# Two groups of two graphs ahead of fifteen groups of four in a five-engine graph kernel

## What is computed

```python
# per graph: x [128,128], adj [128,128]
e      = leaky_relu((x * a_0) @ x.T, 0.2)
scores = where(adj == 1, e, -9e15)
y      = layernorm(x + softmax(scores) @ x)
h      = y @ W_loop.T
g      = h @ Wg_loop.T
vals   = (h + b_loop) * sigmoid(g + bg_loop)
out    = layernorm(y + relu(adj.T_is_1 @ vals))
```

## Time and profile before

| | us |
|---|---|
| median of 3 runs | 109.68 |
| lowest and highest run | 109.47, 110.07 |
| the profiled execution, its own time | 109.15 |
| its span, first to last instruction | 107.4 |
| first real product's weight load | 5.28 |
| first score work on DVE (relu of group 0) | 7.12 |
| last product of the neighbour sums ends | 101.3 |
| mean granted TensorE clock, share of full | 0.99 |

### The profile page before, as it was taken

One profiled execution on the slowest core, in us unless ns is written; L12 is line 12 of the kernel. 1 busy time (PEld: TensorE's weight loads), 2 busy tenths in 40 slices (PEclk: granted clock), 3 DMA queues, 4 the chain that ended last, 5 costly groups with the idle time before them and its releaser, 6 DMA issues.

```text
span 107.4 us, 2765 instructions
## 1 busy us (share of the span) xinstructions
PE 97.9 (91%) x677; PEld 89.4 (83%) x684; DVE 94.4 (88%) x380; ACT 87.1 (81%) x217; POOL 81.0 (75%) x158
## 2 busy tenths in 40 slices
PE   6998999999999999999999999999999999799600
PEld 6986787889999999999999999999999999677400
DVE  0159999999998999997989999999799999987990
ACT  3159968999999999699999999888998889868100
POOL 5025555597588879999989899998979898986760
PEclk9999999999999999999999999999999999999995
DMA  0899999999910093707893304620200303331524
GB/s 15 307 407 367 373 350 297 352 350 388 330 53 0 5 294 95 195 0 201 278 312 97 98 9 113 180 72 26 73 27 6 98 6 98 98 98 46 156 77 124
DMA packets 22531, 17.36 MB, mean 162 GB/s; under 512 B 1265, under 2 KB 18418, under 8 KB 22514
## 3 DMA queue, kind: packets, MB, share of 16 engines
...
q10 hardware_dynamic: 288, 0.26, 0.8%
...
## 4 chain that ended last, share of the span: by engine, by line
POOL 38%; DVE 23%; issue 18%; PE 14%; ACT 3%; POOLq 1%; DVEq 0%; ACTq 0%
POOL rs L707 9%; POOL cent L740 8%; POOL rs L743 7%; DVE nscore L936 5%; DVE res L947 5%; PE p_ag L1038 4%; PE p_hg L1111 3%; DVE rel L918 2%; POOL minus L704 2%; POOL out_s L753 2%; POOL rs L731 2%; PE p_e L1054 2%; POOL rs L702 2%; DVE out_s L1005 2%; POOL y L722 2%
## 5 line engine op out<-in xcount | busy, mean ns | idle before, releaser
L1111 PE MATMUL p_hg<-w_both,y_t 128*128 128x256 f32 x128 | 30.6, 381 | 0.9 <-ACT y_t L871 0.9
L1111 PEld LDWEIGHTS p_hg<-w_both,y_t 128*128 128x128 f32 x128 | 23.0, 190 | 3.8 <-ACT y_t L871 1.3
L830 ACT ACTIVATE prob<-nscore,nmax 128x128 f32<-128x128 f32 x64 | 20.2, 396 | 1.0 <-DVE nmax L936 1.0
L947 DVE SCALAR_TENSOR_TENSOR res<-p_o,rz,inputs 128x128 f32<-128x128 f32 x64 | 18.0, 344 | 1.3 <-ACT y L847 0.6
L1083 PE MATMUL p_o<-inputs,prob_t 128*128 128x129 f32 x128 | 17.2, 276 | 0.2 <-DVE res L947 0.2
L1083 PEld LDWEIGHTS p_o<-inputs,prob_t 128*128 128x128 f32 x128 | 15.9, 191 | 1.0 <-issue 0.7
L707 POOL TENSOR_TENSOR rs<-rs,minus_half 128x4 f32<-128x4 f32 x16 | 16.6, 1037 | 0.0
L1132 PE MATMUL p_ag<-vals,mask 128*128 128x128 f32 x116 | 15.4, 275 | 0.2
L1132 PEld LDWEIGHTS p_ag<-vals,mask 128*128 128x128 f32 x116 | 14.8, 191 | 0.4
L1054 PE MATMUL p_e<-inputs,xat 128*128 128x128 f32 x104 | 14.2, 281 | 0.2 <-DVE nmax L936 0.2
L879 ACT ACTIVATE th<-p_hg 128x256 f32<-128x256 f32 x32 | 11.7, 384 | 3.3 <-PE p_hg L1111 3.3
...
## 6 DMA issues: line engine op xcount, KB each, us to landing
inputs<-x_t SPq DMA_DIRECT2D x16, 256.0 KB, 5.6
inputs<-x SPq DMA_DIRECT2D x16, 256.0 KB, 6.1
inputs<-adj_rows SPq DMA_DIRECT2D x15, 256.0 KB, 5.6
out<-out_s SPq DMA_DIRECT2D x14, 256.0 KB, 2.3
...
inputs<-adj_rows ACTq DMA_DIRECT2D x1, 256.0 KB, 4.4
...
```

The costliest lines, as they stand in the source:

```text
L830: nc.scalar.activation(prob[:, k, i], nscore[:, k, i], ACT.Exp, scale=-1.0, bias=nmax[:, k, i:i + 1]).then_inc(exp_done, 1)
L947: nc.vector.scalar_tensor_tensor(out=res1[:, k, i], in0=p_o[:, i // 2, i % 2, 0:P], scalar=rz[:, k, i:i + 1], in1=x_s(g)[:, i, 0:P], op0=A ...
L1111: last = nc.tensor.matmul(p_hg[:, i], y_t[:, g % 2, i], w_both[:], start=True, stop=True)
```

## The change

The groups get a table of sizes: two groups of two graphs, then fifteen of four, 17 in all. Everything that was `G * g` becomes `START[g]`; a small group uses one half of `p_hg` and of `p_ag` (group 0 the first, group 1 the second), and one half of `p_o`, so that `attend:1` doesn't wait for `residual1:0`. The rings stay at 16 graphs. `absent` gets blocks of 2, 2, 4 and then 8 graphs, `mask` keeps blocks of 8. The first adjacency goes from ACT's queue to SP's, right behind the first turned x. PE warms with eight products, not ten. The arrays of turned x and adjacency are laid out in memory row by row (a row of one partition holds all graphs), not group by group. Of the tables: POOL writes y for 10 graphs (11 before), ACT for 27 (26), DVE for 27 (as before); ACT weighs 36 graphs (32), POOL 24 (24), DVE 4 (8). All five orders are new.

```diff
-SPLIT = (14, 15)
+SIZES = [2] * 2 + [4] * 15
+START = [sum(SIZES[:g]) for g in range(len(SIZES) + 1)]
+HALVES = [(0, 1) if n == G else (g % 2,) for g, n in enumerate(SIZES)]
+ABSENT_BLOCKS = [2] * 2 + [4] + [8] * 7
+MASK_BLOCKS = [8] * 8
+SPLIT = (len(SIZES) - 2, len(SIZES) - 1)
...
-WEIGHED_BY = "vvppppppssssssss"
-RELU_BY = "vvvvssssssssssss"
-TURNED_BY = "vvvsssssssssssss"
-Y_BY = ["vvsp"] * 11 + ["vsss"] * 5
-OUT_BY = ["pppp"] * 10 + ["vvss"] * 4 + ["vvvv"] * 2
+WEIGHED_BY = "vvppppppsssssssss"
+RELU_BY = "vvvvvssssssssssss"
+TURNED_BY = "vvvvsssssssssssss"
+Y_BY = ["vs"] * 2 + ["vvsp"] * 10 + ["vsss"] * 5
+OUT_BY = ["pp"] * 2 + ["pppp"] * 9 + ["vvss"] * 4 + ["vvvv"] * 2
...
     "tensor": """
-        products:0 products:1 turn_probs:0 products:2 products:3 turn_probs:1 attend:0 mix_weights:0 products:4
+        products:0 products:1 turn_probs:0 products:2 turn_probs:1 attend:0 products:3 attend:1 turn_probs:2
+        mix_weights:0 products:4 attend:2 turn_probs:3 turn_y:0 products:5 turn_probs:4 gates:0 attend:3 products:6
...
-        turn_y:13 attend:15 gates:12 sums:11 gates:13 sums:12 turn_y:14 gates_h0:14 sums:13 gates_h1:14 turn_y:15
-        sums_h0:14 gates_h0:15 gates_h1:15 sums_h1:14 sums_h0:15 sums_h1:15
+        gates:11 turn_probs:16 attend:15 turn_y:13 sums:11 gates:12 attend:16 gates:13 turn_y:14 sums:12 gates:14
+        sums:13 turn_y:15 sums:14 gates_h0:15 gates_h1:15 turn_y:16 sums_h0:15 gates_h0:16 sums_h1:15 gates_h1:16
+        sums_h0:16 sums_h1:16
...
     "scalar": """
-        absent:0 absent:1 exp:0 absent:2 mask:0 exp:1 exp:2 absent:4 relu_s:4 exp:3 exp:4 turned_probs_s:3 y_s:0
+        absent:0 absent:1 exp:0 absent:2 exp:1 mask:0 absent:3 exp:2 mask:3 evac_weights:0 absent:5 exp:3 y_s:0 exp:4
...
-        mask:14 tanhs:13 finish_s:10 turned_y:14 finish_s:11 tanhs_h0:14 y_s:15 tanhs_h1:14 turned_y:15 finish_s:12
-        tanhs_h0:15 finish_s:13 tanhs_h1:15
+        mask:13 tanhs:13 turned_y:14 mask:15 finish_s:11 tanhs:14 y_s:15 turned_y:15 finish_s:12 y_s:16 tanhs_h0:15
+        tanhs_h1:15 turned_y:16 finish_s:13 finish_s:14 tanhs_h0:16 tanhs_h1:16
...
     "vector": """
-        weigh_v:0 weigh_v:1 relu_v:0 scores:0 relu_v:1 scores:1 turned_probs_v:0 prepare_w:0 relu_v:2 scores:2
-        relu_v:3 turned_probs_v:1 scores:3 residual1:0 stats1:0 turned_probs_v:2 scores:4 residual1:1 stats1:1 y_v:0
-        scores:5 residual1:2 stats1:2 y_v:1 scores:6 residual1:3 values:0 stats1:3 y_v:2 residual1:4 stats1:4 y_v:3
+        weigh_v:0 weigh_v:1 relu_v:0 scores:0 relu_v:1 scores:1 turned_probs_v:0 relu_v:2 residual1:0 turned_probs_v:1
+        scores:2 stats1:0 prepare_w:0 relu_v:3 turned_probs_v:2 scores:3 y_v:0 residual1:1 relu_v:4 stats1:1 scores:4
+        turned_probs_v:3 y_v:1 residual1:2 scores:5 stats1:2 residual1:3 stats1:3 scores:6 y_v:2 residual1:4 values:0
+        stats1:4 scores:7 residual2:0 y_v:3 residual1:5 stats2:0 values:1 stats1:5 y_v:4 scores:8 residual2:1 values:2
...
     "gpsimd": """
-        weigh_p:2 weigh_p:3 weigh_p:4 weigh_p:5 weigh_p:6 norm1:0 y_p:0 norm1:1 weigh_p:7 y_p:1 norm1:2 y_p:2 norm1:3
-        y_p:3 norm1:4 y_p:4 norm2:0 norm1:5 norm2:1 y_p:5 norm1:6 norm2:2 norm1:7 y_p:6 norm2:3 norm1:8 y_p:7 y_p:8
-        norm2:4 norm1:9 norm2:5 norm1:10 y_p:9 y_p:10 norm2:6 norm1:11 norm2:7 norm1:12 norm1:13 norm2:8 norm1:14
-        norm2:9 norm2:10 norm2:11 norm1:15 norm2:12 norm2:13 norm2_h0:14 norm2_h1:14 norm2_h0:15 norm2_h1:15
+        weigh_p:2 weigh_p:3 weigh_p:4 norm1:0 weigh_p:5 norm1:1 weigh_p:6 weigh_p:7 norm1:2 y_p:2 norm1:3 y_p:3
+        norm1:4 y_p:4 norm2:0 norm1:5 norm2:1 y_p:5 norm1:6 norm2:2 norm1:7 y_p:6 y_p:7 norm2:3 norm1:8 y_p:8 norm2:4
+        norm1:9 norm2:5 y_p:9 norm1:10 norm1:11 y_p:10 norm2:6 y_p:11 norm2:7 norm1:12 norm1:13 norm2:8 norm2:9
+        norm1:14 norm2:10 norm2:11 norm1:15 norm2:12 norm1:16 norm2:13 norm2:14 norm2_h0:15 norm2_h1:15 norm2_h0:16
+        norm2_h1:16
...
     "sync": """
-        load_scores:0 load_scores:1 load_scores:2 load_scores:3 load_weights:0 load_scores:4 load_values:0
+        load_scores:0 load_scores:1 load_scores:2 load_values:0 load_scores:3 load_scores:4 load_values:1
+        load_weights:0 load_scores:5 load_scores:6 load_values:2 load_scores:7 load_values:3 load_values:4
...
-                sp.dma_start(xt(g).rearrange("p g d -> p (g d)"), x_t[g]).then_inc(xt_loaded[g], 16)
-                if g:
-                    sp.dma_start(adj_s(g).rearrange("p g d -> p (g d)"), adj_rows[g]).then_inc(adj_loaded[g], 16)
+                sp.dma_start(xt_all[:, graphs(g)], x_t[:, graphs(g)]).then_inc(xt_loaded[g], 16)
+                sp.dma_start(adj_all[:, graphs(g)], adj_rows[:, graphs(g)]).then_inc(adj_loaded[g], 16)
...
-            nc.scalar.dma_start(adj_s(0).rearrange("p g d -> p (g d)"), adj_rows[0]).then_inc(adj_loaded[0], 16)
...
-            for i in range(10):
+            for i in range(8):
...
                 if g >= 1:
-                    pe.wait_ge(r1_done, G * g)
+                    alone = SIZES[g] < G and SIZES[g - 1] < G
+                    pe.wait_ge(r1_done, START[g - 1] if alone else START[g])
...
-        "x": x, "x_t": rows_of_groups(np.swapaxes(np.asarray(x), 1, 2)), "adj": adj,
-        "adj_rows": rows_of_groups(adj), "a_0": L0_gnn_a_0,
+        "x": x, "x_t": np.transpose(np.asarray(x), (2, 0, 1)), "adj": adj,
+        "adj_rows": rows(adj), "a_0": L0_gnn_a_0,
```

More of the change, by code:

```diff
@@ L37 @@
+MASK_BLOCKS = [8] * 8
[5 more added lines that the diff above has]
+OUT_BY = ["pp"] * 2 + ["pppp"] * 9 + ["vvss"] * 4 + ["vvvv"] * 2
 ORDER = {
     "tensor": """
-        products:0 products:1 turn_probs:0 products:2 products:3 turn_probs:1 attend:0 mix_weights:0 products:4
-        turn_probs:2 attend:1 turn_probs:3 products:5 attend:2 turn_y:0 turn_probs:4 products:6 attend:3 gates:0
@@ new lines @@
+        turn_y:1 turn_probs:5 attend:4 gates:1 products:7 turn_y:2 turn_probs:6 sums:0 attend:5 products:8 turn_y:3
+        turn_probs:7 gates:2 sums:1 turn_y:4 attend:6 products:9 sums:2 gates:3 attend:7 turn_probs:8 products:10
+        sums:3 gates:4 turn_y:5 attend:8 turn_probs:9 products:11 sums:4 turn_y:6 gates:5 attend:9 turn_probs:10
+        products:12 sums:5 gates:6 turn_probs:11 turn_y:7 attend:10 products:13 turn_y:8 gates:7 attend:11 products:14
+        turn_probs:12 sums:6 gates:8 sums:7 turn_y:9 turn_probs:13 attend:12 products:15 sums:8 gates:9 turn_y:10
@@ L539, in groups_of @@
             if stage[-3:] in ("_h0", "_h1"):
-                by = stage[-4]
-                if stage.startswith("finish_"):
-                    return [g for g in SPLIT if by in OUT_BY[g][half(int(stage[-1]))]]
                 return SPLIT
-            if stage in ("gates", "tanhs", "values", "sums", "residual2", "stats2", "norm2", "store"):
+            if stage in ("gates", "tanhs", "values", "sums", "residual2", "stats2", "store"):
                 return [g for g in range(n_groups) if g not in SPLIT]
-            if stage in PAIRED:
-                return PAIRED[stage]
+            if stage == "norm2":
+                return [g for g in range(n_groups) if g not in SPLIT]
+            if stage == "absent":
+                return blocks_of(ABSENT_BLOCKS)
+            if stage == "mask":
+                return blocks_of(MASK_BLOCKS)
             if stage in ("load_weights", "load_others", "prepare_w", "mix_weights", "evac_weights"):
@@ L1151, with rows @@
     from concourse.bass_utils import run_bass_kernel_spmd
[L1153 to L1155 removed]
+    def rows(a):
+        return np.swapaxes(np.asarray(a), 0, 1)
     def turned(a):
```

533 lines of the change are left out of this document (270 added, 263 removed).

## The result

The changed kernel takes 110.19 us (median of 20 runs, 109.42 to 113.45), the kernel before 109.60 us beside it (20 runs, 109.11 to 110.07). The ratio is 1.0053, 95% interval 1.0033 to 1.0073. The forecast was 109.5 us and no change; the kernel is slower by half a per cent. The changed kernel was profiled twice, and the two executions differ: the first took 111.25 us and shows PE's clock falling to half between 14 and 18 us; the second, 109.93 us, the same kernel run again (e1), doesn't, and its rows stand here unless said otherwise. The ratios leave slow executions out, here the four above 111 us.

The account below looks back on a forecast made before the run. Three trains, PE, DVE and POOL, were taken to bound the kernel together, each within about 1 us. Front 0.0, POOL 0.0, tail -0.2 gave 108.95 us profiled; 0.53 more made the median 109.5, range 108.1 to 110.6 (8 in 10).

Parts of the forecast that it names:

- Adjacency on SP's queue: Start, loads: first adjacency issued second on SP's queue moves later issues back; cost 0, bounds -0.2 to +0.4 us.
- The third group: Front: its turned x lands about 5.9 us, relu of group 2 near 8.8; DVE idle 0.9 us, bounds 0.4 to 1.4.
- PE's paragraph: PE before the gapless middle: starts 0.83 us earlier, expected ahead by 0.6 us, bounds 0 to 1.4; added penalties cost 0.1.
- The third rival: PE's early matmuls, 5.69 to 12 us, stay at the lower clock: +1.7 us, 111.2 us; chance 0.04.
- First relu: DVE's first relu, after the first group's scores: starts at 5.75 us, 1.37 us earlier than 7.12.
- DVE idle by 0.9: DVE ahead of group 2's relu: idle about 0.9 us, bounds 0.4 to 1.4, relu starting near 8.8 us.
- Front sum 0.0: DVE's account until 16 graphs have statistics: -1.37 earlier start, +0.9 idle, +0.45 fixed costs, together 0.0 us.
- POOL, 3.1 us more work against 2.8 us earlier: POOL's train: 3.1 us added work, statistics some 2.8 us earlier, 0.3 us less waiting; sum 0.0, bounds -1.2 to +1.1.
- 30 to 31: Sign on POOL: `norm2:0` starts at 30 to 31 us, with POOL packed from there.
- Tail, -0.5 for the covered wait and +0.3 for ACT's finishes: Kernel's end: `sums:14` covers PE's wait before gates, -0.5 us; two finishes ahead of ACT's tanh, +0.3; sum -0.2.
- the covered wait: Tail on PE: `sums:14` between `turn_y` and its gates covers a 0.92 us wait; -0.5 us taken.
- Queue 0: Moving the first adjacency from ACT's to SP's queue: cost 0, bounds -0.2 to +0.4 us.

Follow-up runs that it names:

- e17: The kernel before with only the first adjacency moved to SP's queue, ten warming products kept; ratio 0.9945 to the kernel before.
- e8: The kernel before with the first adjacency on SP's queue and eight warming products instead of ten; ratio 0.9940 to the kernel before, 108.91 us.
- e3: The changed kernel with `absent` in blocks of 2, 2, 4, 4, 4 and then 8 graphs; ratio 0.9989 to the kernel before, median 109.46 us.
- e2: The changed kernel with turned x and adjacency laid out in memory group by group again; ratio 1.0069 to the kernel before.
- e7: The changed kernel with PE's two early waits filled by four products of the zero tile each; ratio 1.0053 to the kernel before.
- e9: e3 with ten warming products instead of eight; ratio 1.0052 to the kernel before.
- e5: e3 with one y each of groups 9, 10 and 11 moved from POOL to ACT; ratio 1.0013 to the kernel before.
- e6: e3 with the first tanh of group 16 ahead of `finish_s:14` in ACT's order; ratio 0.9985 to the kernel before.
- e18: e6 with `gates_h0:15` ahead of `sums:14` on PE, as in the kernel before; ratio 1.0041 to the kernel before.

## Why the prediction was wrong

Going by ratios the change takes apart so: queue -0.55% (e17), eight warming products 0 (e8), the split with its orders, tables and layout +0.5% (e3 against e8), blocks of 8 +0.7% (e1 against e3). Together that is +0.6%, which is e1's own ratio and so no check of the parts; the result above was 0.53%.

- **The step that failed** is "Adjacency on SP's queue" together with "The third group", where adjacency was looked at for `absent:0` and, as a bound, for `absent:2`. `ABSENT_BLOCKS` was not followed to its fourth entry, the first of eight graphs. PE's paragraph, "ahead by 0.6, bounds 0 to 1.4", had no wait at the penalties of group 3; there was one of 1.37 us, 0.5 to 0.6 us of it on the path (e3). The prediction counted the bytes ahead of the third group's turned x, but not the issues ahead of the adjacency of group 4. No rival had it either. The third rival, the clock, was placed in the first 12 us; it fell at 14, and only in some executions.
- **First relu** at 5.75: it was 5.18, and 5.94 where the first products still ran at 1.2 GHz (e2, e7). The forecast had priced the passes at the slow pace; at that pace the relu came 0.19 us later than forecast. The operand came earlier than reckoned (weighed from 3.51, not from 4.03), but warming ends at 4.4 all the same.
- **DVE idle by 0.9** before group 2, start near 8.8: 1.04 and 8.55. Right. The text took row 29.51 of the earlier trace rows for 16 graphs; it is the statistics of the first 20, and its successor in the changed kernel is at 30.70 (e3: 30.16).
- **Front sum 0.0**: right once the blocks are undone. In e3 the last norm is at 94.61, 0.11 from before, with the first relu 2.06 us earlier. The split's own cost is what eats that: with ten warming products in both, the split costs 1.07% (e9 1.0052 against e17 0.9945). That e3's median, 109.46 us, meets the forecast of 109.5 is in part luck: the queue's -0.55% and the split's +0.5%, neither of which was in the sum, cancel.
- **POOL, 3.1 us more work against 2.8 us earlier**: the start of `norm2:0` was 30.55, inside "30 to 31", and the added work real (83.0 against 81.0 us busy, 2.0 more instead of 3.1), but it priced a train that doesn't set the end (e5):

```profile
30.55 0.19 POOL L769 TENSOR_SCALAR rs<-st 128x2 f32<-128x2 f32 x1 [0.69 <-DVE st L1053]
```

- **Tail, -0.5 for the covered wait and +0.3 for ACT's finishes**: it was +0.36 up to the last product and +0.08 up to the end of the span. Both parts were right in kind: the first tanh comes 0.99 us later behind the last norm (4.82 us against 98.33 - 94.50 = 3.83; "up to 1.1" was forecast), and e6 regains 0.22 us; the covered wait is worth 0.44 us (e18 against e6; 0.5 was forecast). What the sum lacked is the rest, by an estimate 0.36 + 0.44 - 0.22 = 0.58 us. PE waits 0.65 us in front of `sums_h0:15` (97.57), where the kernel before, whose first gates stand ahead of the sums, has no wait; that this is the missing term isn't shown.
- **Queue 0**: alone, in the kernel before, it gains 0.55%. ACT's table load and `absent:0` in e17, and then in the kernel before:

```profile
1.16 1.28 ACT L885 ACT_TABLE_LOAD   x1 [1.16 <-PEq L1172]
...
4.88 0.63 ACT L784 ACTIVATE absent<-inputs 128x512 bf16<-128x512 int32 x1 [2.22 <-DMA inputs<-adj_rows]
```

```profile
1.64 1.28 ACT L886 ACT_TABLE_LOAD   x1 [1.64 <-PEq L1173]
...
5.59 0.63 ACT L784 ACTIVATE absent<-inputs 128x512 bf16<-128x512 int32 x1 [2.45 <-DMA inputs<-adj_rows]
```

  The block is ready 0.7 us earlier, but in the kernel before it was ready too, at 5.59 + 0.63 = 6.22 us, ahead of the penalties' load at 6.59. And the two profiles don't show the gain ahead of the last product: the last norm is at 94.59 in e17 and 94.50 before. They show 0.20 us behind it (2.53 against 2.73 us). The rest of the 0.6 us, by which a typical execution of the kernel before is slower than its profiled one, stands in no trace. The Trainium skill (DMA: Bandwidth & Descriptors, Issuing engines are not separate DMA queues) says that a second issuing engine saves only the issue itself; the runs agree, and ACT, the second engine, paid for that saving with a table load that starts at 1.64 instead of 1.16 us.

Two readings of the prediction were off without harm: PE is 91% busy in the earlier trace rows, not among "between 75 and 88%", and weighing 256 columns took 0.35 us, not 0.27.

What stays open: the split's 0.5% (between the profiled spans of e8 and e3, 107.20 and 107.57 us, 0.14 us lie ahead of the last norm and 0.23 behind it, and e6 has 12.71 us from there to the end against 12.73 in e8, yet its ratio is still 0.9985); where the queue's gain comes from; and what makes single executions lose the clock. Undoing the queue in the changed kernel wasn't tried, nor issuing the adjacency of group 4 earlier with the block left whole.

**The best version** is the kernel before with the first adjacency on SP's queue (e17, or e8 with eight warming products): 0.994, 108.9 to 109.0 us, faster than both.
